# Attention over eight query tiles: tile order 5 2 4 3 7 0 6 1 in place of 0 to 7, and value products sorted inside a group

## What is computed

```python
q = l2norm(q) * q_scale; k = l2norm(k) * k_scale          # layers 1 and 3
sim = einsum('bhid,bjd->bhij', q, k) * SCALE + attn_bias  # 16 heads, one shared k and v, one null key ahead
sim = where(causal, neg, sim)                             # query i sees keys 0..i
attn = softmax(sim, axis=-1)
out = einsum('bhij,bjd->bhid', attn, v) @ Wout            # then a layer norm
```

## Time and profile before

| | us |
|---|---|
| runs of the kernel | 2263.55, 2246.25, 2251.49; median 2251.49 |
| span of the profiled execution | 2243.8 |
| PE, DVE, ACT, POOL busy in it | 1965.3, 1693.1, 1338.8, 1085.5 |
| additions (CUSTOM_DVE_ANT_0), 768 | 617.8 |
| transposes, 3456 | 543.9 |
| value products, 2304 records | 438.9 |

### The profile page before, as it was taken

One profiled execution on the slowest core, in us unless ns is written; L12 is line 12 of the kernel. 1 busy time (PEld: TensorE's weight loads), 2 busy tenths in 40 slices (PEclk: granted clock), 3 DMA queues, 4 the chain that ended last, 5 costly groups with the idle time before them and its releaser, 6 DMA issues. The chain is left out here.

```text
span 2243.8 us, 46782 instructions
## 1 busy us (share of the span) xinstructions
PE 1965.3 (88%) x11698; PEld 1421.4 (63%) x11698; DVE 1693.1 (75%) x4092; ACT 1338.8 (60%) x2911; POOL 1085.5 (48%) x1307
## 2 busy tenths in 40 slices
PE   5999585999999998589999999985796999999988
PEld 4887463666666668566666666675564666666658
DVE  4777867877887785758777877758577888877857
ACT  2222665777776674247676767644565777766754
POOL 0443222666765562306666666623034666666643
PEclk8999697999999999799999999997896999999999
DMA  4630166333333343286777888830464433333333
GB/s 118 203 109 31 42 226 250 104 113 113 113 114 113 106 149 110 82 312 189 236 241 236 244 244 243 271 142 21 148 229 163 131 115 116 108 115 107 107 113 113
DMA packets 220535, 338.75 MB, mean 151 GB/s; under 512 B 25766, under 2 KB 102700, under 8 KB 220364
## 3 DMA queue, kind: packets, MB, share of 16 engines
q1 hardware_dynamic: 220364, 336.85, 47.3%
HBM read 250.62 MB, written 102.91 MB: 158 GB/s over the span
## 5 line engine op out<-in xcount | busy, mean ns | idle before, releaser
L1653 POOL TENSOR_SCALAR at_row<-at_row,at_inv 128x129 f32<-128x129 f32 (+7 forms) x384 | 715.2, 1862 | 352.9 <-DVE at_inv L1817 347.2
L1864 ACT ACTIVATE at_row<-at_row,at_nmax 128x129 f32<-128x129 f32 (+7 forms) x768 | 595.4, 775 | 231.8 <-DVE at_nmax L1836 230.2
L1836 DVE CUSTOM_DVE_ANT_0 at_row<-at_s,bias,at_row 128x128 f32<-128x128 f32 (+7 forms) x768 | 617.8, 810 | 63.3 <-PE at_s L1764 35.9
L1776 PE MATMUL at_t<-ident,at_row 128*128 128x128 f32 x3456 | 543.9, 280 | 42.6 <-ACT at_pt L1857 37.7
L1776 PEld LDWEIGHTS at_t<-ident,at_row 128*128 128x128 f32 x3456 | 391.4, 141 | 247.9 <-issue 165.7
L1763 PE MATMUL at_s<-k_hh,q_hl 128*128 128x512 f32 (+3 forms) x1152 | 462.2, 401 | 41.9 <-SPq L1721 21.8
L1792 PE MATMUL at_o<-at_pt,v 128*64 128x512 f32 (+3 forms) x2304 | 438.9, 503 | 5.8 <-ACT at_pt L1857 2.5
L1668 DVE COPY at_pt<-at_t 128x128 f32<-128x128 f32 (+3 forms) x576 | 278.5, 484 | 179.6 <-PE at_t L1776 175.7
L1764 PE MATMUL at_s<-k_lp,q_h 65*128 65x512 f32 (+3 forms) x1152 | 392.9, 353 | 0.0
L1857 ACT ACTIVATE at_pt<-at_t 128x512 f32<-128x512 f32 (+2 forms) x576 | 306.7, 533 | 135.5 <-PE at_t L1776 130.3
L1763 PEld LDWEIGHTS at_s<-k_hh,q_hl 128*128 128x128 f32 x1152 | 224.6, 195 | 76.1 <-DVE at_nmax L1836 32.2
(11 more groups left out here) (249 smaller groups left out, 2863.9 us busy)
## 6 DMA issues: line engine op xcount, KB each, us to landing
q_hl<-q_dram SPq DMA_DIRECT2D x192, 256.0 KB, 4.0
q_dram<-o_in SPq DMA_DIRECT2D x76, 512.0 KB, 3.7
bias<-bands_dram SPq DMA_DIRECT2D x64, 512.0 KB, 5.4
q_h<-q_dram SPq DMA_DIRECT2D x96, 256.0 KB, 4.8
o_dram<-o_sb SPq DMA_DIRECT2D x96, 256.0 KB, 4.3
bands_dram<-brow_dram SPq DMA_DIRECT2D x2, 8192.0 KB, 33.6
bias<-corners_dram SPq DMA_DIRECT2D x256, 64.0 KB, 4.2
bias<-in_fside SPq DMA_DIRECT2D x32, 448.0 KB, 4.8
```

Source lines behind the costliest of these rows:

```text
L1653: return eng.tensor_scalar(cells, cells, inv[:, i:i + 1], None, ALU.mult)
L1776: last = eng.transpose(t_ps[m % NTR][:, c * P:(c + 1) * P], row[:, u % RING, here:here + P], t["ident"][:])
L1836: eng.tensor_tensor_reduce(out=row[:, u % RING, ZERO:ZERO + width], in0=s_ps[u % 2][:, 0:width], in1=bt[:, lo:lo + width], scale=-1.0, sca ...
L1864: eng.activation(cells, cells, ACT.Exp, scale=-1.0, bias=nmax[:, i:i + 1], accum_out=rsum[:, i:i + 1]).then_inc(s["exp"], 1)
```

## The change

A table `TILES` gives the order of tiles, 5 2 4 3 and 7 0 6 1, so that both groups hold 18 key blocks. Inside a group the columns of `at_o` are sorted by tile (`group_tiles`), and a key block's product starts at the first tile that sees it. `group_runs` gives the runs of neighbouring tiles: one for the first group (2 to 5), two for the second (0, 1 and 6, 7), so that group's queries take six DMAs and its output two. Row slots are as wide as their widest tile; the weights `at_pt` have a pitch of 512 throughout. Twelve rows of bias, not 14, are loaded ahead in layer 2; the first queries are loaded together, later; SP gets a semaphore instruction between a wait and the DMAs behind it.

```diff
-HEAD_SLOTS, BIAS_IN_FLIGHT, ROWS_FIRST = 4, 16, 14
+TILES = (5, 2, 4, 3, 7, 0, 6, 1)
+GT = NT // 2
+HEAD_SLOTS, BIAS_IN_FLIGHT, ROWS_FIRST = 4, 16, 12
...
+def tile_of(u):
+    return TILES[(u // 2) % NT]
+def group_tiles(g):
+    return sorted(TILES[g % 2 * GT:(g % 2 + 1) * GT])
+def group_runs(g):
+    tiles = group_tiles(g)
+    starts = [n for n, tile in enumerate(tiles) if n == 0 or tile != tiles[n - 1] + 1] + [GT]
+    return [(tiles[a] * P, a * P, (b - a) * P) for a, b in zip(starts, starts[1:])]
...
-    widths = [((u // 2) % NT + 1) * P for u in range(4 * NT)]
+    widths = [(tile_of(u) + 1) * P for u in range(4 * NT)]
...
-                    if q in (NPAIR - 1, 2 * NPAIR - 1):
...
-                        load_queries(eng, t, s["first"], g, 0)
+                    if q == 2 * NPAIR - 1:
...
+                        for g in range(2):
+                            load_queries(eng, t, s["first"], g, 0)
...
 def load_queries(eng, t, sem, g, pair):
...
-        eng.dma_start(f32(out), t["q_dram"][one, part, :, cols].rearrange("o (s d) i -> d (o s) i", d=DH)).then_inc(sem, 16)
+        for from_, to, n in group_runs(g):
+            eng.dma_start(f32(out[:, :, to:to + n]),
+                          t["q_dram"][one, part, :, from_:from_ + n].rearrange("o (s d) i -> d (o s) i", d=DH)).then_inc(sem, 16)
...
+    def key_blocks(g):
+        return group_tiles(g)[-1] + 1
+    def place_of(u):
+        return group_tiles(u // GU).index(unit(u)[1])
+    slot_sizes = [ZERO + (max(TILES[i // 2], TILES[GT + i // 2]) + 1) * P for i in range(RING)]
...
-        row = sb("at_row", [P, RING, ZERO + S])
-        pt = [sb(f"at_pt{n}", [P, 2, 4 * n * BANK + 3 * NARROW + BANK]) for n in range(2)]
+        row = sb("at_row", [P, sum(slot_sizes)])
+        pt = [sb(f"at_pt{g}", [P, 2, key_blocks(g), BANK]) for g in range(2)]
...
                 def store(place, g):
                     place.wait(eng, "out", g + 1)
+                    eng.sem_inc(s["gate"], 1)
...
-                    blocks = 4 * (g % 2) + 4
+                    blocks = key_blocks(g)
...
-                        i0 = max(0, j - (blocks - 4)) * P
+                        i0 = sum(tile < j for tile in group_tiles(g)) * P
```

More of the change, by code:

```diff
@@ L1216, in _ @@
                 t["q_stored_n"] += 16 * NST
-                eng.wait_ge(s["first"], 96 + (16 * FIRST if bias is None else sum(row_loads(n) for n in range(FIRST))))
+                eng.wait_ge(s["first"], sum(QUERY_LOADS) + (16 * FIRST if bias is None else sum(row_loads(n) for n in range(FIRST))))
             @block.tensor
@@ L1569, in load_bias @@
     else:
-        tile = (n // 2) % NT
+        tile = tile_of(n)
         width = (tile + 1) * P
@@ L1633, in unit @@
     def unit(u):
-        tile = (u // 2) % NT
+        tile = tile_of(u)
         return u % U // (2 * NT), tile, u % 2, (tile + 1) * P
+    def key_blocks(g):
[3 more added lines that the diff above has]
+    slot_sizes = [ZERO + (max(TILES[i // 2], TILES[GT + i // 2]) + 1) * P for i in range(RING)]
+    slot_at = [sum(slot_sizes[:i]) for i in range(RING)]
     with tensors(nc) as (sb, ps):
@@ L1647, in null_cell, with weights, cells @@
         def null_cell(u, n=1):
-            return row[:, u % RING:u % RING + n, ZERO - 1]
+            at, size = slot_at[u % RING], slot_sizes[u % RING]
+            return row[:, at:at + n * size].rearrange("p (n c) -> p n c", n=n)[:, :, ZERO - 1]
+        def weights(u):
+            at = slot_at[u % RING] + ZERO
+            return row[:, at:at + unit(u)[3]]
+        def cells(u):
+            at = slot_at[u % RING] + ZERO
+            return row[:, at - 1:at + unit(u)[3]]
         def scale_row(eng, u):
-            i = u % RING
-            cells = row[:, i, ZERO - 1:ZERO + unit(u)[3]]
-            return eng.tensor_scalar(cells, cells, inv[:, i:i + 1], None, ALU.mult)
+            return eng.tensor_scalar(cells(u), cells(u), inv[:, u % RING:u % RING + 1], None, ALU.mult)
         def evacuate(eng, turn, u, copy, parity, name):
@@ L1662, in evacuate @@
                 at, blocks = pieces[m % NPC]
[L1663 to L1668, removed]
+                col = place_of(u) * P
+                copy(pt[u // GU % 2][:, u % 2, at:at + blocks, col:col + P],
                      t_ps[m % NTR][:, 0:blocks * P].rearrange("p (c i) -> p c i", i=P)).then_inc(s[name], 1)
@@ L1774, in transposes @@
                         for c in range(blocks):
-                            here = ZERO + (at + c) * P
-                            last = eng.transpose(t_ps[m % NTR][:, c * P:(c + 1) * P], row[:, u % RING, here:here + P],
+                            here = (at + c) * P
+                            last = eng.transpose(t_ps[m % NTR][:, c * P:(c + 1) * P], weights(u)[:, here:here + P],
                                                  t["ident"][:])
@@ L1859, in exponent @@
                 def exponent(turn, u):
[L1860 removed]
                     i = u % RING
[L1862 removed]
                     turn.wait(eng, "biased", u + 1)
[L1864 removed]
+                    eng.activation(cells(u), cells(u), ACT.Exp, scale=-1.0, bias=nmax[:, i:i + 1],
                                    accum_out=rsum[:, i:i + 1]).then_inc(s["exp"], 1)
                 def output(turn, g):
[L1868 removed]
+                    turn.wait_loads(eng, f"o{g % 2}", OUTPUT_STORES[g % 2] * NGRP // 2, OUTPUT_STORES[g % 2] * (g // 2 + 1))
                     turn.wait(eng, "pv", g + 1)
```

53 lines of the change are left out of this document (23 added, 30 removed).

## The result

| kernel | median us (runs) | against before |
|---|---|---|
| before | 2251.0 (4) | |
| after | 2228.3 (2224.8 to 2230.0, 4) | 0.989 [0.986, 0.992] |

The change saves 22.8 us, 1.0%. The forecast was 2200, a saving of 51: the sign was right, the size was less than half of it. One profile stands for each kernel, and the one of before is among the shorter of its executions (2241 to 2264 us, at a mean granted clock of 0.940 to 0.947 where it is on record), so a few microseconds between two profiles can be chance.

A forecast was written before the change was run, and what follows sets the result against it. It took DVE's idle time, 5.68 us a pair, much of it waits for PE, as what could be won. From 2243.8: -72 for pairs, +18 for layer 2's split, +3 for starts and ends, with 7.7 to the median: 2200, range 2168 to 2244.

The forecast's parts named there:

- pairs: 48 pairs of heads in the three attention stages: 1.5 us less each by balanced groups, -72 us.
- split in layer 2: SP's queue in layer 2: the second group's extra DMAs delay the ninth unit's bias, 2.5 us more a turn, +18 us.
- starts and ends: Attention stages' first and last groups: later start, fewer but less covered products at the end, +1 a stage, +3 us.
- I take 1.5 us a pair: Gain per pair of heads, set near the waits' sum of 1.8 us less; kept range 0.6 to 2.2.
- I take PE by starts: PE's work per pair, counted from instruction starts instead of busy time: 24 us, against DVE's 22.9.
- hand sum of DVE's waits: DVE's waits in a pair, estimated step by step: 3.3 us before, 1.5 after the new order.
- rival (a): DVE's waits in the pairs only move elsewhere: 0.6 us a pair gained, 2243 us in all; chance 0.15.
- price of an issue: SP's queue in layer 2: 0.78 us per query issue, so the second group's longer set adds 2.9 us.
- A query load is waited for a group later: SP's queue in layers 1 and 3: the second group's extra DMAs have cover and cost nothing; without it 2.9 us.
- Rival (b): SP becomes the bound in layer 2; 1 KB-row issues taking twice as long add 33 us; up to 2276; chance 0.08.
- Rival (c): Query and output transfers in half-length rows: DMA share 0.79 to 0.9, later bias in layer 2, +12, 2212 us; chance 0.08.
- Two key blocks more: Value products on PE: key blocks per pair from 12 to 14, 2 x 0.05 us extra a pair, inside the 1.5.

The follow-up runs named there:

- e4: Kernel after, with each group's queries and outputs moved as one run of 512 columns (wrong queries, same work): 2204.0 us, 0.980 of before.
- e6: Kernel after, scaling only the first 129 columns of each row, on DVE and POOL: 2200.2 us in one run, layer 3's twelve pairs 319.3.
- e5: Kernel after, leaving out value products of odd key blocks but a group's last: 2159.0 us in one run, layer 3's twelve pairs 305.4.
- e3: Kernel after with tile order 2 0 3 1 and 6 4 7 5, mixed inside unbalanced groups: 2244.6 us, 0.997 of before.
- e7: Kernel after, with queries and outputs kept in DRAM in group order, so each group is one run: 2209.8 us, 0.980 of before.
- e8: Like e7, but the second group's DMAs cut by side, 64 partitions with rows of 2 KB: 2225.6 us, 0.988 of before.
- e1: Kernel after with the tile table set back to the old order 0 to 7: 2256.5 us, 1.0025 of before.

## Why the prediction was right or wrong

The forecast's terms against what the spans show. The pairs' value is taken where the split doesn't disturb: layers 1 and 3 of the kernel after, layer 2 of e4 (45 pairs, without the first of each layer).

| term | forecast us | measured us |
|---|---|---|
| pairs | -72 | -41 (-7.0, -17.8, -16.2) |
| split in layer 2 | +18 | +22 (after less e4) |
| starts and ends | +3 | 0 (+10.3 in the three first pairs, -10.4 elsewhere) |
| sum | -51 | -19 |

- The step that failed is "I take 1.5 us a pair": over 45 pairs it was 0.9. Under it lie two sentences. One is "PE reads as busy for 27.2, but that hides what its matmuls overlap, so I take PE by starts", which gave 24 us a pair. The busy time was the better number: 27.05 in layer 3 before, 26.6 after, 26.5 in e6, where DVE had 2.5 us less to do. It left 1.2 us a pair of idle time to win. Of that 0.7 was won, and another 0.5 because the busy time itself got shorter, which the forecast had no term for; the steady pair gained 0.8. The other is the hand sum of DVE's waits, 3.3 to 1.5. It treated each wait as the effect of one step of PE, while PE, by e5 and e6, was the slower engine all through. So the wait taken from the two-block copy came back before the four-block copy, 1.08 us a pair where the sum had 0.1. That is rival (a), the waits move, in part: it got 0.15 at 0.6 a pair, and 0.9 was measured (41/45). The removed wait had "a single cause, which goes", as the argument against (a) said, but the time came back elsewhere all the same.
- The bounds of that term were 0.6 and 2.2, so the result lay in them, and the whole in the range (2168 to 2244).
- The forecast's sum has no term for the granted clock, and one was missing: in layer 1 the clock's falls and the stalls ahead of them took some 6 us, 0.3% of the whole, and in layer 2 before and after have three falls each where e3, e4 and e7 have none.
- Layer 2: the price of an issue was right (0.78, 3.0 for 2.9), and the sum near, 22 for 18, but by luck. The ninth unit waits 2.2 us a turn and not 4.3, 0.5 more than before for the 2.5 forecast; the rest of the 22 is waits at the 25th unit, for tile 5's bias and for queries, and the clock. "A query load is waited for a group later", costed at nothing in layers 1 and 3, was true there; layer 2 has 12.3 us of such waits (6.6 before), and the forecast has no term for them. Rival (b), SP the bound, was right in its claim and wrong in its reason: by the gaps SP is 91% full in layer 2, where (b) counted 48 of 58 us (83%), but issues in 1 KB rows didn't take twice as long, 0.78 us each against 1.42/2 = 0.71 in 2 KB rows. That issue time goes with the count of rows is not borne out either: a bias DMA has 128 rows too and takes 0.33 us.
- Rival (c), the transfers: DMA's share stayed at 0.78, no 0.9, and landing got shorter (3.0 us for loads of 128 KB, 5.0 for those of 256 before). Its premise fell. e8 leaves 7.9 us to the shorter rows, 6 of them time of SP.
- Two key blocks more, forecast at 0.1 us a pair: PE is busy with the value products of layer 3's twelve pairs for 108.9 us after and 108.8 before, so they cost nothing that the windows show. PE as a whole is busy for less, 319.0 for 324.6, by its transposes. That their records overlap more was read off and not tested by a run.
- The reciprocal waits 1.08 us a pair for ACT (1.2 forecast, 0.90 before): right. Twelve pairs of layer 1 in 325 us: wrong (337); that layer 3 has 324.8 is no hit, it started from 338.7 and not from 343.
- Starts: each first pair holds a whole group of 18 blocks where it held one of 10, which I had at 1 us and which costs 2.5, 4.2 and 3.5; the ends give it back.

## What to carry to other kernels

Before adding up the waits of one engine that a change removes, look at the idle time of the engine it waits for: here it was 1.2 us a pair and not 5.7, and the gain in layer 3 came to 1.16, 0.7 of it idle time and the rest records that overlapped more. A busy share of 95% is not to be explained away before an experiment has lightened that engine. When an order is changed for balance, store the data in the new order too: one run cut in two cost half of the gain, 12.2 of layer 2's 20.1 us through the number of DMAs that one queue issues (e8 less e7). And ask of a term that came out right whether its time was spent where the sum had it: layer 2's +22 for +18 was not.

## What the runs showed of the hardware

- One stall of DVE, 1.75 us, with PE busy 0.28 us of two, was followed by some 7 us at a granted clock of 0.50, in the middle of a stage whose twelve pairs have a mean of 0.98. Two stalls of 1.84 and 1.75 us in layer 3 of before were followed by none. Two falls of this kind made e1's two pairs 4.8 us longer.
- Four `q_hl` loads in a row took SP 0.78 us each, gaps included, with 128 rows of 1 KB, and 0.63 with 64 rows of 2 KB, of the same bytes; bias DMAs followed each other every 0.5 to 0.7 us.
- A scaling of 129 columns on DVE took 0.60 us in layer 3 of the kernel after, where each of the twelve had one of POOL's scalings beside it. In layer 3 of before the median was 0.27 us for the four without and 0.59 for the eight with one (0.27 to 1.03). In e6, where POOL's are short too, it was 0.28 with and without.
